# Two-bank row maxima and a new tile order in the first rounds of a four-block attention kernel

## What is computed

```python
# blocks 0 and 1 (8 heads of 16 channels), for each image and head
xn = group_norm(x)
q, k, v = split(xn @ w_qkv)                       # 1024 x 16 each
p = softmax(q @ k.T * 16 ** -0.5, axis=-1)        # 1024 x 1024
x = x + concat_heads(p @ v) @ w_out + b_out       # block 1 adds to xn
# blocks 2 and 3: the same with one head of 128 channels
```

## Time and profile before

| | |
|---|---|
| median of 3 runs | 2293.45 us (2292.23 to 2298.7) |
| the profiled execution | 2305.12 us |
| its span, first to last instruction | 2303.3 us |
| TensorE matmuls busy | 2156.2 us (94%) |
| VectorE busy | 1688.6 us (73%) |
| ScalarE busy | 1471.8 us (64%) |
| VectorE, tile maxima (line 1073), 2048 | 1284.1 us, 680 ns each |
| mean granted TensorE clock | 0.981 |

### The profile page before, as it was taken

How to read it: one execution, slowest core, us unless ns; L and a number is a source line. 1 busy time by engine, 2 the same in 40 slices (tenths; PEclk the granted TensorE clock), 3 DMA queues, 4 the chain that set the end, 5 groups by cost and what they waited for, 6 DMA issues and landing times.

```text
span 2303.3 us, 41605 instructions
## 1 busy us (share of the span) xinstructions
PE 2156.2 (94%) x16748; PEld 1154.2 (50%) x16748; DVE 1688.6 (73%) x3104; ACT 1471.8 (64%) x1722; POOL 379.9 (16%) x517
## 2 busy tenths in 40 slices
PE   5999999999999999999999999999999988999999
PEld 3443343434633367333663347633475334745888
DVE  6898898889688866787678876788767965672433
ACT  1566677767477754778448774587646875477555
POOL 3101101220121211112110211202111030021121
PEclk7899999999999999999999999999999999999999
DMA  5403132231221303031130402304031040000000
GB/s 135 83 12 88 35 75 63 41 79 16 55 48 43 52 20 78 16 66 29 49 63 2 93 1 52 61 2 92 2 83 20 2 88 6 6 6 1 6 6 19
DMA packets 48591, 97.46 MB, mean 42 GB/s; under 512 B 7824, under 2 KB 10640, under 8 KB 48272
## 3 DMA queue, kind: packets, MB, share of 16 engines
q1 hardware_dynamic: 48400, 94.81, 20.0%
HBM read 55.98 MB, written 37.75 MB: 41 GB/s over the span
## 4 chain that ended last, share of the span: by engine, by line
PE 72%; DVE 18%; issue 4%; ACT 3%; DMA 1%; POOL 1%; SPq 0%; POOLq 0%; ACTq 0%; DVEq 0%
PE outs L1335 17%; PE work L1281 15%; DVE part_max L1073 13%; PE outs L1375 10%; PE pairs L1353 8%; PE pairs L1309 6%; PE pairs L1197 5%; PE work L1206 5%; PE pairs L1206 3%; ACT probs L962 2%; PE work L1203 1%; DVE o_turn L1085 1%; DVE stats L1011 1%; DMA q_stack<-shift_parts 1%; DVE neg_max L1105 1%
## 5 line engine op out<-in xcount | busy, mean ns | idle before, releaser
L1073 DVE TENSOR_REDUCE part_max<-work 128x1 f32<-128x512 f32 x2048 | 1284.1, 680 | 244.2 <-PE work L1281 239.2
L962 ACT ACTIVATE probs<-pairs 128x1024 f32<-128x1024 f32 x1024 | 1004.4, 1022 | 374.0 <-PE pairs L1309 361.6
L1281 PE MATMUL work<-k_stack,q_stack 62*128 62x512 f32 x2048 | 729.1, 463 | 32.7 <-DVE part_max L1073 25.7
L1309 PE MATMUL pairs<-q_stack,k_stack 64*128 64x512 f32 x2048 | 607.7, 441 | 20.7 <-DMA q_stack<-shift_parts 10.4
L1335 PE MATMUL outs<-probs,v_heads 128*32 128x256 f32 (+1 forms) x5448 | 591.8, 499 | 6.2 <-DVE o_turn L1085 6.1
L1281 PEld LDWEIGHTS work<-k_stack,q_stack 62*128 62x128 f32 x2048 | 317.4, 188 | 555.8 <-DVE part_max L1073 408.1
L1105 DVE TENSOR_REDUCE neg_max<-pairs 128x1 f32<-128x1024 f32 x128 | 156.6, 1223 | 254.1 <-PE pairs L1353 254.0
L1309 PEld LDWEIGHTS pairs<-q_stack,k_stack 64*128 64x128 f32 x2048 | 274.6, 187 | 76.3 <-ACT probs L962 51.8
L969 ACT ACTIVATE probs<-pairs,neg_max 128x1024 f32<-128x1024 f32 x128 | 142.8, 1115 | 241.2 <-DVE neg_max L1105 241.2
L1375 PE MATMUL outs<-v_full,probs 128*128 128x128 f32 x2048 | 259.6, 280 | 4.8 <-issue 4.8
L1375 PEld LDWEIGHTS outs<-v_full,probs 128*128 128x128 f32 x2048 | 242.4, 192 | 37.5 <-issue 34.3
(11 more groups left out here) (126 smaller groups left out, 1122.0 us busy)
## 6 DMA issues: line engine op xcount, KB each, us to landing
k_scratch<-parts SPq DMA_DIRECT2D x64, 256.0 KB
q_scratch<-parts SPq DMA_DIRECT2D x64, 256.0 KB
k_stack<-k_scratch SPq DMA_DIRECT2D x64, 256.0 KB, 7.1
q_stack<-q_scratch SPq DMA_DIRECT2D x64, 256.0 KB, 9.7
k_stack<-k_scratch SPq DMA_DIRECT2D x64, 128.0 KB, 8.4
q_stack<-q_scratch SPq DMA_DIRECT2D x64, 128.0 KB, 10.6
q_stack<-shift_parts SPq DMA_DIRECT2D x256, 4.0 KB
tmp<-x SPq DMA_DIRECT2D x7, 512.0 KB, 3.4
```

The source lines that it names most:

```text
L962: nc.scalar.activation(probs[:, plan.prob[u], 2 * n:2 * n + 2, :], pairs[:, plan.half["pair", t], :, :], ACT.Exp, scale=HEAD_SCALE).then_i ...
L1073: nc.vector.tensor_reduce(part_max[:, r % 2, column:column + 1], bank_of(("tile", r, n)), AX_X, ALU.max, negate=True).then_inc(tile_max, 1)
L1281: nc.tensor.matmul(bank_of(("tile", r, n)), qs[rows, i, a, heads, P * t:P * (t + 1)], ks[rows, i, keys, heads, :], start=True, stop=True). ...
L1309: last = nc.tensor.matmul(pairs[:, plan.half["pair", t], half, :], ks[rows, i, key // QT, first + n, P * (key % QT):P * (key % QT + 1)], q ...
```

## The change

The change has three parts, all for tiles of rounds 0 to 20 (`JOINED_ROUNDS = 21`).

First, one maximum for two tiles: the odd tiles of a group of four (n % 4 equal to 1 and 3, the two key halves of the head on the second row half) go to banks beside each other, and VectorE takes both maxima with one instruction over 128 x 2 x 512 elements, after the later of them. The even tiles keep an instruction each. So of four maxima three are left, one of them twice as wide.

Second, the banks: tile n % 4 = 1 always goes to bank 1, and while joined tiles are near in the order everything else in `work` goes to bank 0 or 2, whichever was given out longer ago. The turn n mod 3 is gone for all items; away from joined tiles the bank given out longest ago is taken, which is the same turn.

Third, the slots that ran `HALVES_PATTERN` (their first tile always belongs to a round below 21) run "TPTTCPTV" and multiply the values whole.

```diff
--- before.py
+++ after.py
@@ -74,6 +74,7 @@
 
 
     FIRST_TILES = 40
+    JOINED_ROUNDS = 21
 
     def __init__(self):
         self.beats, self.head_beat, self.full_beat = [], {}, {}
@@ -290,6 +291,7 @@
     PATTERNS = {0: "PCPV", 1: "TPCPV", 2: "TPCTPV", 3: "TPCTTPV", 4: "TPCTTPTV"}
     SHIFT_LAST = True
     HALVES_PATTERN = "TPTPCUTTV"
+    JOINED_PATTERN = "TPTTCPTV"
     CHUNK_PATTERNS = {0: "PPCV", 1: "TPPCV", 2: "TPTPCV", 3: "TPTPTCV", 4: "TPTCUTPTV"}
 
     def beat(self, b):
@@ -327,7 +329,7 @@
                 shifts = []
             if len(groups) == 4 and steps == self.PATTERNS[4] and all(
                     len(self.tiles.get(a, [])) >= 4 for a in (b - 1, b + 1)):
-                steps = self.HALVES_PATTERN
+                steps = self.JOINED_PATTERN if self.tiles[b][0][0] < self.JOINED_ROUNDS else self.HALVES_PATTERN
             for step in steps:
                 if step == "P" and pairs:
                     order.append(pairs.pop(0))
@@ -376,13 +378,19 @@
     def full_values(self, n):
         return [("pv", n // 2, QT * (n % 2) + k) for k in range(QT)]
 
+    def joined(self, item):
+
+        return item[0] == "tile" and item[1] < self.JOINED_ROUNDS and item[2] % 2 == 1
+
     def follows_full(self, u):
         b = self.head_beat[u // STAGE_SLOTS, u % STAGE_SLOTS]
         return b > 0 and self.beats[b - 1][0] == "full"
 
     def count(self):
 
-        self.bank, self.before, held, n = {}, {}, {}, 0
+        self.bank, self.before, held = {}, {}, {}
+        self.maximum, maxima = {}, 0
+        released, opened = [0] * WORK_BANKS, None
         self.use, self.takes, self.chunks = {}, {}, []
         self.gn, self.ln, self.roots, self.tile_nth = {}, {}, {}, {}
         self.norms_before = {}
@@ -402,7 +410,7 @@
             if (c[0] == "shift" or c[0] == "chunk" and c[1] in COLUMNS) and (
                     follows[0] == "values" or follows in self.by_columns):
                 self.by_columns.add(c)
-        for item in self.order:
+        for position, item in enumerate(self.order):
             kind = item[0]
             if kind == "tile":
                 self.tile_nth[item] = len(self.tile_nth)
@@ -410,10 +418,22 @@
             if kind == "pair":
                 self.rows_first[item] = 1 - rows
             if self.in_work(item):
-                bank = n % WORK_BANKS
-                n += 1
+                outer = opened is not None or any(self.joined(c) for c in self.order[position:position + 12])
+                banks = range(0, WORK_BANKS, 2) if outer else range(WORK_BANKS)
+                if self.joined(item) and item[2] % 4 == 1:
+                    banks = [1]
+                bank = min(banks, key=lambda b: released[b])
                 self.bank[item], self.before[item] = bank, held.get(bank)
                 held[bank] = item
+                released[bank] = position
+                if self.joined(item) and item[2] % 4 == 1:
+                    opened = item
+                elif self.joined(item):
+                    released[1] = position
+                    self.maximum[opened], opened = maxima, None
+                if kind == "tile" and opened != item:
+                    self.maximum[item] = maxima
+                    maxima += 1
             elif self.in_pairs(item):
                 self.half[item] = ring % 2
                 ring += 1
@@ -1067,13 +1087,21 @@
                                             ).then_inc(taken_by["dve"], 1)
 
                 def tile_maximum(r, n):
-                    t = plan.tile_nth["tile", r, n]
-                    dve.wait_ge(tile_full, t + 1)
+                    both = plan.joined(("tile", r, n))
+                    if both and n % 4 == 1:
+                        return
+                    dve.wait_ge(tile_full, plan.tile_nth["tile", r, n] + 1)
                     column = TILES // 2 * (n % 2) + n // 2
-                    nc.vector.tensor_reduce(part_max[:, r % 2, column:column + 1], bank_of(("tile", r, n)),
-                                            AX_X, ALU.max, negate=True).then_inc(tile_max, 1)
+                    if both:
+                        low, high = sorted((plan.bank["tile", r, n - 2], plan.bank["tile", r, n]))
+                        nc.vector.tensor_reduce(part_max[:, r % 2, column - 1:column + 1],
+                                                work[:, low:high + 1, :],
+                                                AX_X, ALU.max, negate=True).then_inc(tile_max, 1)
+                    else:
+                        nc.vector.tensor_reduce(part_max[:, r % 2, column:column + 1], bank_of(("tile", r, n)),
+                                                AX_X, ALU.max, negate=True).then_inc(tile_max, 1)
                     if n == TILES - 1:
-                        dve.wait_ge(tile_max, t + 1)
+                        dve.wait_ge(tile_max, plan.maximum["tile", r, n] + 1)
                         nc.vector.tensor_reduce(neg_max[:, r % 2, :],
                                                 part_max[:, r % 2, :].rearrange("p (n a) -> p n a", a=2),
                                                 AX_X, ALU.min).then_inc(max_ready, 1)
@@ -1185,7 +1213,7 @@
                     if before is None:
                         return
                     if before[0] == "tile":
-                        pe.wait_ge(tile_max, plan.tile_nth[before] + 1)
+                        pe.wait_ge(tile_max, plan.maximum[before] + 1)
                     elif before[0] == "shift":
                         pe.wait_ge(*taken(*before))
                     else:
```

## The result

| | before | after |
|---|---|---|
| median | 2296.07 us (4 runs, 2292.23 to 2304.1) | 2354.24 us (4 runs, 2351.52 to 2358.44) |
| ratio | | 1.0248, 95% interval 1.0228 to 1.0267 |
| the profiled execution | 2305.12 us | 2351.52 us |
| its span | 2303.3 us | 2349.7 us |

The kernel became 58 us slower. The forecast was 2356 us. The two profiled executions lie only 46 us apart: when slot 159 starts the kernel after is 55.8 us behind, at 624.67 us against 568.88 us, and it stays 53 to 56 us behind up to 1900 us. Another 7.2 us of the distance go between 1885 and 1995 us. There the execution of before ran 13.6 us at 1.2 GHz and that of after 3.4 us. By an estimate (half the rate for 10.2 us) that explains about 5 us.

The account below looks back on a forecast made before the run. TensorE's order was taken to bound the plain slot, so its waits for banks count. The terms summed to 62.8 us, taking the profiled 2305.1 to 2368 and the median to 2356 us; range 2310 to 2385.

Parts of the forecast that it names:

- (a): Halves slot after halves slot, 69: 42 plain lose 0.19 each, 8.0 us; the other 27 lose 0.1 each, 2.7 us.
- (b): Chunk slot after chunk slot, 27: next group's second tile waits for the join, 0.9 us each, 24.3 us.
- (c): Halves slot after a chunk slot, 19: waits for the join and the first tile's maximum, 0.75 each, 14.3 us.
- (d): Chunk slot after a halves slot, 17: whole values give the join its time, loss 0.05 each, 0.9 us.
- (e): Slots 148 to 158, pairs across slots, lose 8 us; twelve slots with or following five or six tiles, 3.6 us.
- (f): The 40 tiles ahead of the first slot: a group takes 2.8 us instead of 2.40; ten groups, 4 us.
- given back: Pairs that wait for the DMA of a shift will find it landed; some 3 us regained.
- cheaper waits: Rival, whole kernel: the mechanism holds but the terms are at their low bounds, 2320 us; chance 0.23.
- banks don't bind: Rival, nearly all slots: joins end ahead of the next group's second tile, so faster, 2276 us; chance 0.06.
- that rival: Rival, chunk slots and those after them: idle TensorE lowers the clock more often, 20 us more, 2376; chance 0.15.

Follow-up runs that it names:

- e5: Changed kernel with each joined maximum taken over only the first 256 of 512 columns per bank; 2312 us, ratio 1.0067.
- e11: Changed kernel with two late single-bank maxima in place of each joined one, the first bank freed only after the second maximum; 2367 us, ratio 1.0303.
- e2: Changed kernel with joins and bank rule kept, but the old order with halved values in the four-tile slots; 2427 us, ratio 1.0571.
- e7: Changed kernel with the chunk moved behind all tiles and pairs in four-tile chunk slots, then the values whole; 2342 us, ratio 1.0202.
- e3: Changed kernel with new order and bank rule kept, but a maximum of its own for each tile in the old place; 2319 us, ratio 1.0096.
- e1: Changed kernel with the joins and their bank rule taken out, only the new order left; 2303 us, ratio 1.0029.

## Why the prediction was right

By its own steps, with the delay summed over the slots of each kind (profiled executions, start of first tile to start of first tile):

| step | predicted us | measured us |
|---|---|---|
| (a) four tiles after four tiles, 69 | 10.7 | 4.6 |
| (b) chunk after chunk, 27 | 24.3 | 21.1 |
| (c) four tiles after chunk, 19 | 14.3 | 12.2 |
| (d) chunk after four tiles, 17 | 0.9 | -3.8 |
| (e) slots 148 to 158 | 8 | 5.9 |
| (e) slots with other numbers of tiles, 15 | 3.6 | 12.7 |
| (f) up to the start of slot 1 | 4 | 3.1 |
| given back | -3 | (in (a)) |
| sum | 62.8 | 55.8 |

**Right in mechanism, and near in size: (b), (c) and the plain part of (a).** The working of (b) gave 0.94 us from the rows of one slot; 0.92 to 0.94 was measured in thirteen slots of the kind. Three that carry an output projection too lost 0.62, since its own wait covered a part; four that begin with tile 0 lost 1.8 to 1.9, and the slots behind them changed by -0.18 to 0.05. That made 21.1 of 24.3. e5 and e11 show that the length of the join sets it, e2 and e7 that the distance from t3 to the next t1 does. In (c) the typical slot takes 3.15 us; 3.21 had been worked out before the allowance for the pair, which was not needed. The slot it replaces took 2.61 and not the 2.52 of the sum, which is that of a plain one. So the typical loss was 0.54, not 0.75. Plain slots measured 2.70 against 2.71.

**Near in size: (f).** From the tiles ahead of the first slot, t3's load, t0's maximum, the load of t1 (with t2), the join, and the same again:

```profile
52.30 0.28 PEld L1309 LDWEIGHTS work<-k_stack,q_stack 62*128 62x128 f32 x1 [0.73 <-DVE part_max L1101]
...
53.30 0.68 DVE L1101 TENSOR_REDUCE part_max<-work 128x1 f32<-128x512 f32 x1
53.43 0.28 PEld L1309 LDWEIGHTS work<-k_stack,q_stack 62*128 62x128 f32 x2 [0.85 <-DVE part_max L1097]
...
54.90 1.22 DVE L1097 TENSOR_REDUCE part_max<-work 128x2 f32<-128x1024 f32 x1
55.04 0.28 PEld L1309 LDWEIGHTS work<-k_stack,q_stack 62*128 62x128 f32 x1 [0.73 <-DVE part_max L1101]
...
56.17 0.29 PEld L1309 LDWEIGHTS work<-k_stack,q_stack 62*128 62x128 f32 x2 [0.85 <-DVE part_max L1097]
```

From one t1 to the next lie 56.17 - 53.43 = 2.74 us, where 2.8 was worked out and 2.40 was the old value. But e3 lost 3.7 us up to slot 1 without any join, so there the bank rule alone is enough, and the join that the working names is not needed for the loss. Under the rule t0 gets t2's bank, only two tiles back, and in this stretch at 1.2 GHz a tile takes longer (785 ns) than a maximum (680 ns).

**Mis-sized: the terms around shifts.** (b) counted chunk slots with a shift like all others, at 0.9 us. In a chunk slot that begins with tile 0, after another chunk slot, the loss was 1.8 to 1.9 us, twice that. (In plain slots it was 0.03, where (a) had 0.1.) The shift and the next t0, in such a slot of the changed kernel:

```profile
226.46 0.49 PE L1309 MATMUL work<-k_stack,q_stack 62*128 62x512 f32 x1
...
227.74 0.28 PE L1295 MATMUL work<-avg,neg_max 128*16 128x128 f32 x1 [0.54 <-DVE part_max L1101]
...
228.87 0.49 PE L1309 MATMUL work<-k_stack,q_stack 62*128 62x512 f32 x1 [0.31 <-DVE part_max L1097]
```

Both wait, the shift for t2's maximum (0.54 us of idle TensorE) and t0 for the join (0.31 us), on top of t1's wait at the slot's start. The prediction named the banks of tiles only and never asked which bank the other users of `work` would get; half of what lies between e1 and e3 is the same, 9.3 of 18.9 us. The parts of the change do not simply add: a plain slot with a shift takes 3.66 us in e3 and 3.09 in the changed kernel, where t2's maximum has no t1's ahead of it.

**Mis-sized: slots of five and six tiles**, 12.7 us instead of 3.6. There the pairs lie across the slots, and VectorE had a queue of norm statistics besides; one slot (57) alone lost 2.9 us and the next 1.4. The execution of after ran at 1.2 GHz from 264.2 to 274.4 us, in just these two, and from 284.6 to 291.4; how much of the 12.7 us is the clock's, no run separates. The 3.6 was a guess without a row.

**Wrong sign: (d) and the rest of (a).** -3.8 us instead of 0.9, and -3.6 instead of 2.7 in the 27 slots of (a) that are not plain. These come with the order and not with the joins: e1 has -5.5 and -4.7 in the same slots. Ahead of an output projection the longer slot gives VectorE the time for its transposition, and pairs find their shift landed: TensorE's waits for the DMAs of a shift fell from 3.8 to 1.1 us (the -3 of the prediction, which is in (a) here). Slots 48 and 49 alone are 3.8 us, and the clock of the one profiled execution of before has a part in them; by e1's median, 7 us above before, part of this is chance.

It is luck in part that the median came within 2 us of the forecast. By slots the terms missed by 9.1 us one way (slots with other numbers of tiles) and by 16.1 the other. The sum was 62.8 us, where 55.8 was measured at slot 159 and 58.2 by the medians. The 4.6 us that are left were made up in part by the median of before, 2296.07 with the fourth execution and not the 2293.45 that the forecast started from.

The change split by runs, in the order in which its parts are added: the new order 0.9 us of delay at slot 159, the bank rule 18.9 more, the joined maxima 36.0 more. The prediction put nearly all behind the order's 10.7 on the join; a third of the loss comes with the bank rule even without joins. That a tile waits for a bank, where it does so, and the largest terms are what the runs confirm. Of the rivals, cheaper waits are excluded by slots of 4.27 us. That banks don't bind is excluded for chunk slots by the same, and for plain slots it was nearly true: there the join's end falls together with t1. The clock fell a little more (1.2 GHz for 78 us of the changed kernel's first 600, 65 before), 7 us of effect at most if the work halves its rate there, not the 20 of that rival, though TensorE idled more in the whole third.

## What to carry to other kernels

Before two small instructions are joined, ask who waits for the first one's input buffer: a join frees both buffers at the end of both, and with three buffers in rotation that can cost the waiting engine more (here 0.93 us in each of a run of chunk slots) than the join saves (0.06 us). Read the timeline of one slot of each kind and find the distance between the last producer of a joined pair and the next user of its buffer. Set it against the time from that producer's start to the end of the joined instruction (in chunk slots 1.24 us against 410.88 - 408.87 = 2.01). If it is shorter, the engine that fills the buffers stalls, however busy the other looked. And when a buffer rule changes, list every user of the pool, the rare ones too.

## What the runs showed of the hardware

A maximum over two PSUM banks in one instruction took 1218 ns and one over a single bank 681 ns, and back to back the joined form took 0.06 to 0.07 us less of VectorE than two single ones (e11 against the changed kernel, in slot after slot). A tile that waits loads its weights about 0.05 us after the maximum that frees its bank has ended (409.75 to 409.80 and 410.88 to 410.93 in the chunk slot shown). More idle time of TensorE did not lower the granted clock between 300 and 400 us: it was 1.00 at 91% busy as at 95%.
